# Edge stage of a graph network kernel: 16-bit table halves, narrower target ranges, bias as a product, comparisons a unit ahead

## What is computed

```python
p1 = tanh(h @ pp_W1 + pp_b1) @ pp_W2 + pp_b2
inter = concat(p1[src], p1[dst]) @ pi_W1 + pi_b1      # then @ pi_W2 + pi_b2, then @ pi_W3
i1 = einsum('ecb,eb->ec', inter.reshape(E, 64, 8), basis)
i1 = tanh(i1 @ ii_W1 + ii_b1) @ ii_W2 + ii_b2
out = segment_sum(i1, dst)
```

## Time and profile before

| what | us |
|---|---|
| median of 3 runs | 8050.49 (8045.1 to 8051.35) |
| profiled execution, its own time | 8058.17 |
| its span, first to last instruction | 8056.5 |
| edge stage, first to last addition into aggT | 315.2 to 3987.7 |

### The profile page before, as it was taken

How to read it: one execution, slowest core, us unless ns; L and a number is a source line. 1 busy time by engine, 2 the same in 40 slices (tenths; PEclk the granted TensorE clock), 3 DMA queues, 4 the chain that set the end, 5 groups by cost and what they waited for, 6 DMA issues and landing times. The chain is left out here.

```text
span 8056.5 us, 132776 instructions
## 1 busy us (share of the span) xinstructions
PE 7250.3 (90%) x44520; PEld 4945.0 (61%) x44520; DVE 3022.3 (38%) x4630; ACT 2022.9 (25%) x3278; POOL 1563.6 (19%) x1655
## 2 busy tenths in 40 slices
PE   4688888888888888888779999999999999999999
PEld 2577777777777777777645555555555555555554
DVE  5566666666666666666540000011100000011000
ACT  3344444444444444444300000000000000000000
POOL 2334433443443344334200000000000000000000
PEclk9799999999999999999889999999999999999999
DMA  3688888888888888888758787877788888888776
GB/s 103 164 213 213 217 210 214 214 217 211 214 216 213 213 214 217 211 214 214 174 200 281 268 281 268 280 269 279 272 295 289 295 289 290 293 290 293 266 267 228
DMA packets 828957, 1927.15 MB, mean 239 GB/s; under 512 B 66366, under 2 KB 123134, under 8 KB 828862
## 3 DMA queue, kind: packets, MB, share of 16 engines
q1 hardware_dynamic: 775564, 1816.94, 74.5%
q0 software_dynamic: 52352, 108.63, 4.3%
q10 hardware_dynamic: 946, 0.26, 0.0%
HBM read 1752.16 MB, written 173.46 MB: 239 GB/s over the span
## 5 line engine op out<-in xcount | busy, mean ns | idle before, releaser
L1199 PE MATMUL ps_a<-ring,table 128*128 128x448 fp8e4 x19208 | 3656.3, 353 | 42.8 <-DVE table L105 42.8
L1199 PEld LDWEIGHTS ps_a<-ring,table 128*128 128x128 f16 x19208 | 1881.8, 98 | 1793.4 <-DVE table L105 44.4
L593 ACT CAST unit<-ps_c 128x490 fp8e4<-128x490 f32 (+1 forms) x2548 | 1641.0, 662 | 1994.7 <-PE ps_c L734 1976.0
L560 POOL DMA_INDIRECT gathered<-u_source,plan x1576 | 1486.8, 943 | 2326.9 <-PE ps_u L756 1773.9
L734 PE MATMUL ps_c<-cell_hot,lane_hot 128*128 128x490 f16 x2548 | 889.2, 370 | 490.5 <-DVE cell_hot L643 490.5
L643 DVE TENSOR_SCALAR cell_hot<-iota_n,cell 128x490 f16<-128x490 f16 x2548 | 728.3, 343 | 378.4 <-PE ps_c L734 378.3
L1023 ACT COPY agg<-ps_a 128x448 f32<-128x448 f32 x196 | 104.3, 532 | 2930.3 <-PE ps_a L1199 2930.3
L773 PEld LDWEIGHTS ps_m<-M_sb,z 128*128 128x128 f32 x6272 | 810.2, 192 | 34.5 <-issue 0.3
L773 PEld LDWEIGHTS ps_m<-M_sb,x_sb 128*128 128x128 f32 x6272 | 810.0, 192 | 13.1
L997 POOL COPY hst<-h 128x896 f32 x28 | 26.4, 943 | 3925.8 <-PE ps_t L1211 2463.0
L773 PE MATMUL ps_m<-M_sb,x_sb 128*128 128x64 f32 x6272 | 784.7, 268 | 0.0
(11 more groups left out here) (185 smaller groups left out, 3302.1 us busy)
## 6 DMA issues: line engine op xcount, KB each, us to landing
ring<-counts SPq DMA_DIRECT2D x392, 1848.0 KB, 7.1
ring<-counts SPq DMA_DIRECT2D x196, 1792.0 KB, 7.0
basis<-in_basisT SPq DMA_DIRECT2D x198, 1024.0 KB
x_sb<-in_basisT SPq DMA_DIRECT2D x198, 1024.0 KB
counts<-unit SPq DMA_DIRECT2D x196, 784.0 KB
dst_all<-in_dst_seq SPq DMA_DIRECT2D x198, 512.0 KB
gathered<-u_source,plan POOLq DMA_INDIRECT x1576
window<-u_target SPq DMA_DIRECT2D x198, 64.0 KB
```

The costliest lines, as they stand in the source:

```text
L560: pool.indirect_dma_start(gathered[q][:, i, :], None, Us, bass.IndirectOffsetOnAxis(ap=T["plan"][:, at:at + 1], axis=0)).then_inc(S[f"rows ...
L593: nc.scalar.copy(unit[q][:, :, BD * i:BD * i + n], got[:, :, 0:n], saturate=False).then_inc(S["emptied"], 1)
L1199: last = mm(ps_a[:, b, 0:BC].rearrange("p (u c) -> p u c", u=BU), table[n % 2][:, k, :], cells, start=(k == 0), stop=(k == TILES - 1))
```

## The change

- The tables Us and Ud hold each vector as two f16 halves (high part, and the rest times 2048); the row is the same 512 bytes. VectorE writes the lower halves in the preparation (`lower`).
- A unit's 1024 edges are two half groups of 512, each with its own base and a range of 64 targets (W was 128). The window has 64 nodes by 2 parts on 128 partitions; from_node holds 1 or 1/2048 in f16. Targets relative to the base are made once (dst_local, f16), in the preparation. The gathered tiles are multiplied by id_hi (identity) and id_lo (identity/2048).
- The bias is one product of 33 rows into ps_m ahead of the message products; the tanh reads PSUM.
- cell_hot has 13 buffers in place of 7, and the comparisons are made a unit ahead.
- SP loads dst_all and the windows ahead of the basis, with a semaphore of their own. TensorE's, VectorE's and ScalarE's orders are new. The addition into aggT is two of 64 columns, each with its own base.
- The general path, not shown, is changed alike. Padding edges point to node 12500.

New in `prepare` beside what is shown: small vectors on VectorE ahead of its first work (parity of the partition, bias rows), and a wait for the load of all targets.

```diff
-RING = 7
-W = P
+W = 64
 ET = 8
+HT = ET // 2
 EG = ET * P
+EH = EG // 2
...
+    Us = nc.dram_tensor("u_source", (NP, 4 * D), F16, kind="Internal").ap()
+    Ud = nc.dram_tensor("u_target", (NP + W, 4 * D), F16, kind="Internal").ap()
+    dst_local = nc.dram_tensor("dst_local", (EP + 2 * EG,), F16, kind="Internal").ap()
...
+        uv = sb("uv", [P, GT, 2, 2, 2, D], F16)
...
+                sp.wait_ge(S["low"], 4 * g + 4)
+                sp.dma_start(Us.rearrange("(k p) d -> p k d", p=P)[:, bass.ds(g * GT, GT), :], uv[:, :, 0, :, :, :].rearrange("p k s h d -> p k (s h d)")).then_inc(S["st"], 16)
+                sp.dma_start(Ud[0:NP, :].rearrange("(k p) d -> p k d", p=P)[:, bass.ds(g * GT, GT), :], uv[:, :, 1, :, :, :].rearrange("p k s h d -> p k (s h d)")).then_inc(S["st"], 16)
...
+            nc.vector.tensor_tensor(local, targets, targets[:, :, 0].unsqueeze(2).to_broadcast([DP, 4, EH]), ALU.subtract).then_inc(S["local"], 1)
...
+            def lower(g):
+                for b in range(4):
+                    n = cols[b] // P
+                    ks = slice(4 * b, 4 * b + n)
+                    v = psB[:, b, 0:cols[b]].rearrange("p (k h d) -> p k h d", h=2, d=D)
+                    dve.wait_ge(S["tb_ev"], 4 * g + b + 1)
+                    nc.vector.tensor_tensor(rest[:, ks, :, :], v, uv[:, ks, :, 0, 0, :], ALU.subtract).then_inc(S["tb_lo"], 1)
+                    dve.wait_ge(S["tb_lo"], 4 * g + b + 1)
+                    twice = [P, n, 2, D]
+                    ch(nc.vector.tensor_scalar(uv[:, ks, 0, 1, :, :], rest[:, ks, 0, :].unsqueeze(2).to_broadcast(twice), LO, None, ALU.mult))
...
+            for g in range(GROUPS):
+                if g:
+                    dve.wait_ge(S["tp"], 4 * g)
+                centre_and_scale(nc, ch, x_sb[:, g * GT:(g + 1) * GT, :], xc[:, :, :], sq[:, :, :], small, hst[:, :, :],
                                  S["var"], S["root"], g + 1).then_inc(S["h_ready"], 1)
-                assert ch.n == step, ch.n
-            ch = Chain(dve, S["dve"], before + GROUPS * step)
+                if g:
+                    lower(g - 1)
+            lower(GROUPS - 1)
+            dve.wait_ge(S["low"], 4 * GROUPS)
+            dve.wait_ge(S["kept"], 16)
...
-                pe.wait_ge(S["tb_ev"], 4 * g)
+                pe.wait_ge(S["tb_lo"], 4 * g)
...
-        dst_all = two(sb, "dst_all", [P, EG], I32)
-        window = two(sb, "window", [P, 2 * D], F32)
-        from_node = two(sb, "from_node", [P, EG], F32)
+        dst_all = two(sb, "dst_all", [P, EG], F16)
+        window = two(sb, "window", [P, 2, 2 * D], F16)
+        from_node = two(sb, "from_node", [P, EG], F16)
-        gathered = two(sb, "gathered", [P, ET, 2 * D], F32)
+        gathered = two(sb, "gathered", [P, ET, 2, 2 * D], F16)
-        cell_hot = [sb(f"cell_hot{i}", [P, TILES * BD], F16) for i in range(RING)]
+        cell_hot = [sb(f"cell_hot{i}", [P, TILES * BD], F16) for i in range(UB)]
-        ps_w = ps("ps_w", [P, W])
+        ps_w = ps("ps_w", [P, 2, W])
...
-                    base = base_of(sp, g)
+                    bases = [base_of(sp, g, h) for h in range(2)]
                     sp.wait_ge(S["z_done"], 4 * t + 2 * q)
+                    sp.dma_start(dst_all[q][:, :], G["dst_local"][bass.ds(g * EG, EG)].unsqueeze(0).to_broadcast([P, EG])).then_inc(S[f"placed{q}"], 16)
+                    for h in range(2):
+                        sp.dma_start(window[q][:, h, :], Ud.rearrange("n (s d) -> (n s) d", s=2)[bass.ds(bases[h] * 2, 2 * W), :]).then_inc(S[f"placed{q}"], 16)
                     load_basis(sp, g, basis[q], S[f"loaded{q}"])
-                    sp.dma_start(dst_all[q][:, :], dst_seq[bass.ds((g + 1) * EG, EG)].unsqueeze(0).to_broadcast([P, EG])).then_inc(S[f"loaded{q}"], 16)
-                    sp.dma_start(window[q][:, :], Ud[bass.ds(base, W), :]).then_inc(S[f"loaded{q}"], 16)
...
-                        empty(t, q, range(0, 11))
-                        act.wait_ge(S[f"m_bias{q}"], t + 1)
-                        nc.scalar.activation(msg[q][:, :, 0:D], msg[q][:, :, 0:D], ACT.Tanh).then_inc(S[f"tanh{q}"], 1)
-                        empty(t, q, range(11, UB))
+                        empty(t, q, range(0, UB - 1))
+                        act.wait_ge(S["m_done"], 2 + 4 * t + 2 * q + 2)
+                        nc.scalar.activation(msg[q][:, :, 0:D], ps_m[q][:, :, :], ACT.Tanh).then_inc(S[f"tanh{q}"], 1)
+                        empty(t, q, [UB - 1])
...
                 def place_from(t, q):
-                    dve.wait_ge(S[f"loaded{q}"], 64 * t + 64)
+                    dve.wait_ge(S[f"placed{q}"], 48 * t + 48)
                     dve.wait_ge(S[f"u{q}"], 2 * t)
-                    nc.vector.tensor_scalar(from_node[q][:, :], dst_all[q][:, :], T["nodeid"][:, bass.ds(2 * t + q, 1)], None, ALU.is_equal).then_inc(S[f"from{q}"], 1)
+                    nc.vector.tensor_scalar(from_node[q][:, :], dst_all[q][:, :], T["row_node"][:, :], T["row_scale"][:, :], ALU.is_equal, ALU.mult).then_inc(S[f"from{q}"], 1)
...
-                        user = (g, i - RING) if i >= RING else (g - 1, i + RING if i + RING < UB else i)
-                        dve.wait_ge(S["counted"], multiplied(*user))
-                        nc.vector.tensor_scalar(cell_hot[i % RING][:, :], T["iota_n"][:, :], T["cell"][:, bass.ds(g * UB + i, 1)], None, ALU.is_equal).then_inc(S["cells"], 1)
-                def multiply(t, q):
+                        dve.wait_ge(S["counted"], multiplied(g - 1, i))
+                        nc.vector.tensor_scalar(cell_hot[i][:, :], T["iota_n"][:, :], T["cell"][:, bass.ds(g * UB + i, 1)], None, ALU.is_equal).then_inc(S["cells"], 1)
+                def multiply(t, q, h):
+                    n = 4 * t + 2 * q + h
+                    dve.wait_ge(S[f"loaded{q}"], 32 * t + 32)
+                    dve.wait_ge(S[f"u{q}"], 2 * t + h + 1)
+                    dve.wait_ge(S["m_done"], n + 1)
+                    nc.vector.tensor_tensor(z[h][:, :, :], ps_u[h][:, :].unsqueeze(1).to_broadcast([P, 4, 512]), basis[q][:, :, 512 * h:512 * h + 512], ALU.mult).then_inc(S["z_done"], 1)
+                def add(g):
                     for h in range(2):
-                        n = 4 * t + 2 * q + h
-                        dve.wait_ge(S[f"loaded{q}"], 64 * t + 64)
-                        dve.wait_ge(S[f"u{q}"], 2 * t + h + 1)
-                        dve.wait_ge(S["m_done"], n + 1)
-                        nc.vector.tensor_tensor(z[h][:, :, :], ps_u[h][:, :].unsqueeze(1).to_broadcast([P, 4, 512]), basis[q][:, :, 512 * h:512 * h + 512], ALU.mult).then_inc(S["z_done"], 1)
-                def add(g):
-                    base = base_of(dve, g - 1)
-                    dve.wait_ge(S["summed"], g + 1)
-                    dve.wait_ge(S["added"], g)
-                    there = aggT[:, bass.ds(base, W)]
-                    nc.vector.tensor_tensor(there, there, ps_w[0:D + 1, :], ALU.add).then_inc(S["added"], 1)
+                        base = base_of(dve, g - 1, h)
+                        dve.wait_ge(S["summed"], g + 1)
+                        dve.wait_ge(S["added"], 2 * g + h)
+                        there = aggT[:, bass.ds(base, W)]
+                        nc.vector.tensor_tensor(there, there, ps_w[0:D + 1, h, :], ALU.add).then_inc(S["added"], 1)
                 place_from(0, 0)
                 place_from(0, 1)
                 place_lanes(0, 0)
-                for h in multiply(0, 0):
-                    pass
+                place_cells(0, 0, range(UB))
+                for h in range(2):
+                    multiply(0, 0, h)
                 with dve.Fori(0, STEPS) as t:
                     for q in range(2):
                         g = 2 * t + q
                         following = (t, 1) if q == 0 else (t + 1, 0)
+                        place_lanes(*following)
                         place_to(t, q)
-                        place_cells(t, q, range(0, 11))
-                        for h in multiply(*following):
-                            if h == 0:
-                                dve.wait_ge(S["m_done"], 4 * t + 2 * q + 4)
-                                nc.vector.tensor_tensor(msg[q][:, :, 0:D], ps_m[q][:, :, :], T["iib1"][:, :].unsqueeze(1).to_broadcast([P, ET, D]), ALU.add).then_inc(S[f"m_bias{q}"], 1)
                         place_from(t + 1, q)
-                        place_cells(t, q, range(11, UB))
-                        place_lanes(*following)
+                        place_cells(*following, range(0, 4))
+                        multiply(*following, 0)
                         add(g)
+                        place_cells(*following, range(4, 8))
+                        multiply(*following, 1)
+                        place_cells(*following, range(8, UB))
                 add(EGROUPS)
...
-                        mm(ps_c[(UB * q + i) % 2][:, 0:TILES * BD], lane_hot[q][:, i, :], cell_hot[i % RING][:, :], start=True, stop=True).then_inc(S["counted"], 1)
```

(52 more changed lines are left out.)

146 lines of the change are left out of this document (86 added, 60 removed).

## The result

The changed kernel takes **8202.35 us** (median of 4, 8170.1 to 8224.82) where the kernel before takes 8050.92 (8045.1 to 8053.68): 1.0186 times, 95% interval 1.0143 to 1.0229. It is 1.9% slower. I had forecast 7670. The profiled execution took 8224.82 us, its span 8223.1.

What follows compares the result with a forecast made beforehand. The edge stage, bounded by a VectorE chain then TensorE (18.74 us a unit), would become bounded by the store of the counts at 16.6: 8058 - 419 + 38 = 7677, by the median 7670 us; range 7390 to 7890.

Steps and rivals of the forecast that it cites:

- The order of the stage: Edge stage: which engine waits for which in the new order, with the store of the counts ending last.
- 4.75 said: VectorE: second multiplication ends 4.75 us after a unit's last message product, 2.4 us late through the second base read.
- the fast path is taken: Edge stage: half groups fit their range, the widest spanning 37 of 64 targets; chance of failing under 0.01.
- Rival 3: VectorE: from_node waits for its window's load; as the limit 16.6 to 17.5 us a unit, 7760 us; chance 0.14.
- rival 1: Edge stage: the store does not gate, the transfers decide; 15.2 us a unit, 7395 us; chance 0.25.
- TensorE's durations: Edge stage, TensorE: sum 1.07 us, window product 0.22, f16 gather 0.08 each, eight message blocks with counts 8.2.
- the store has landed at T+20.6: Edge stage transfers: store of the counts lands 20.6 us after T, the end of a unit's last message product.
- as today 2 us of idleness cost 0.3 on the mean, I keep 0.3: Edge stage, TensorE's clock: idling 2 to 3 us a unit adds 0.3 us, making 16.3 into 16.6.
- rival 2: Edge stage: clock low for most of each unit; about 8690 us, slower from a mean clock of 0.69 down; chance 0.04.
- From cast 0 to the end of the products are 12.0 us: Edge stage: from ScalarE's released cast 0 to the end of that unit's message products, 12.0 us.
- 16.3 a unit ahead of its clock term: Edge stage: two units take 20.6 + 12.0 = 32.6 us, so 16.3 us each before the clock's 0.3.
- Preparation: Before the edge stage: 38 us more (18 group waits, 15 codes at the end, 5 start), between 10 and 50.

Runs made afterwards that it cites:

- Experiment 9: Changed kernel with each join's window product written four more times (overwritten); 8133.61 us, 1.0107 of the kernel before; the changed kernel rerun beside it took 8187.3.
- experiments 4: Changed kernel's 16-bit data parts with the kernel before's order put back on VectorE, TensorE and ScalarE; 9520.15 us, 1.1841 of the kernel before.
- 6: Changed kernel's data parts in the old order, plus four overwritten window products in each join; 8549.1 us, 1.0627 of the kernel before.
- experiment 10: Changed kernel with store ahead of load, base reads behind lanes and to_node, and preparation's codes ahead of the last lower halves; 7544.8 us, 0.9377.
- Experiment 1: Changed kernel with SP issuing the store of the counts ahead of the load; 8474.54 us, 1.052 of the kernel before.
- 8: Changed kernel with only the base reads moved behind lanes and to_node; executions of 7882.01, 7917.65, 8005.36 and 18880.34 us, no ratio formed.
- 5: Changed kernel with store ahead of load and base reads moved behind lanes and to_node; 7550.42 us, 0.9385 of the kernel before.

## Why the prediction was wrong, step by step

- *The order of the stage* was read rightly: cast 0 waits for the store of the counts, VectorE idles 2.4 us between its additions, the second multiplication ends 4.8 us after the products in most of the units behind a released cast (4.75 said), from_node has no wait that counts, the fast path is taken. Rival 3's mechanism is absent, and rival 1 (the store doesn't gate) is refuted by the 61 waits. (Its 0.83 of 18.7 is 15.6, not 15.4; nothing else hangs on that.)
- *TensorE's durations* were right at the full clock: sum 1.13 us (1.07 said), window product 0.21, message products 1.00 for eight, as before; a gather's product 0.055 apart, where I took 0.08: it is at the low end of my bounds.
- **First failed step: "the store has landed at T+20.6"**, that is 15.85 us after the end of the second multiplication. The cast that waits for it was released 17.4 to 20.5 us after, 18.7 in the mean. I had taken the transfers' work over from a unit of the kernel before, scaled it by bytes, and ended it with the last packet. But the small loads now go first, so that the basis starts 3.3 us after the buffer came free in place of 1.6; gathers that came behind the load now share it; the next unit's load, which at a shorter period is issued before the store has landed, shares its end; and from the last packet to the released cast are 0.7 to 1.0 us, which no row of before showed because nothing waited. 2.9 us in a round of two are 1.4 a unit.
- **Second failed step: "as today 2 us of idleness cost 0.3 on the mean, I keep 0.3"**, and with it rival 2's chance of 0.04. It shows in two places. "From cast 0 to the end of the products are 12.0 us" holds in the quickest units (11.8) but is 13.1 on the mean of 42, since the clock is still low while sum and join run (the sum takes 1.99 us there, 1.13 at the full clock): 0.6 a unit. And 19 of the 61 gated units ran wholly at the lower level. From the released cast to the end of the second multiplication they take 23.5 us where the 42 take 18.2 (of the 8 us that they lose up to the tanh some 2.5 come back behind it, where VectorE is no longer late): 19 x 5.3 / 103 is 1.0 a unit.
- Together: the forecast's 16.3 a unit ahead of its clock term, 1.4 for the landing, 0.6 and 1.0 for the clock, and 0.1 for the second multiplication (5.0 us on the mean of the 42, 4.75 said) are 19.4; measured are 19.37. So the late store took some 280 us of the forecast gain, and the clock, less the 0.3 allowed for it, some 250. Experiment 9 has the same without a wholly slow unit: 18.2 by its round of two, and (18.7 + 18.2) / 2 = 18.4 by the changed kernel's 42, against 16.6.
- Why rival 2 was priced too low: I had counted it as every unit wholly at the lower level; a third of the gated ones were. Its threshold, a mean clock of 0.69, was set for the whole gain to be lost by the clock alone; with the late store 0.80 was enough. The argument against it, that today's pauses leave 0.96, looked at the pause of 2 us (9 us now) and left out what follows it. In the kernel before, f32 joins and a sum of 128 columns run there. The change thins exactly these, and experiments 4 and 6 show what that does: the new data in the old order fall to 0.59, and repeated products bring back 0.86. The Trainium skill (TensorE: Matmul & The Clock Gate, HAM oscillation) describes kernels that pause in each round and swing between the levels; by the 61 gated units, where TensorE pauses up to 9 us, the trace agrees.
- *Preparation*: 38 us forecast, 62.7 measured at the flag's store (310.09 against 247.37), 44 at the first addition, since the way from the flag to that addition is shorter. The start is 7.3 of it (5 said). The end part, 15 said, grew by 23.4; experiment 10 shows 14 of it are the codes' place. The groups between the first and the last square root took 25.5 us each in place of 20.2, six times 5.3 = 32, where I had 18; TensorE waits only 1.74 of it for the lower halves, and its clock from 100 to 200 and from 200 to 300 us was 0.64 and 0.50 (0.91 and 0.65 before). I had charged one wait and left the clock out again.

The sum as it came out: 7670, and 196 x (19.37 - 16.6) = 543 for the stage, and 24 for the preparation beyond its 38 (only 6 of them seen at the first addition): 8219 to 8237, by the profiled execution 8225.

How the loss divides between the late store and the clock is read from the trace and not tested: each of the two lengthens the pause that the other lives on, so mending one alone needn't return its share. Experiment 1 (store early, reads in the way) and 8 (reads hidden, store late) show that neither edit alone brings the forecast gain, 5 that both together do.

## What to carry to other kernels

A change that thins products behind a pause can slow a kernel through its clock: before counting the saved work, look at what TensorE runs right after each of its waits, and whether that stretch was what brought the clock back. Where a wait is forecast that nobody has today, its end can't be read off the old trace's transfers: add the time to the waiter's release, and what the shorter period itself puts into the same queue. Look also at what the change sends earlier than before (here small loads and gathers), since it shares the transfers' time. And try the removal of waits in pairs: store first alone made this kernel slower by 270 us, and with the reads hidden it made it faster by some 350.
